# Attention on one core: VectorE takes the second maximum of a tile directly behind the first, ahead of the first low half

## What is computed

```python
x = x + _L0_xattn_ref(_layernorm(x), ctx_1024, ctx_1024, mask_SxS2_bk1, ...)   # masked
x = x + _L0_ffn_ref(_layernorm(x), ...)          # top 4 of 32 experts and a shared one
x = x + _L1_xattn_ref(_layernorm(x), ctx_1024, ctx_1024, ...)                  # not masked
x = x + _L1_ffn_ref(_layernorm(x), ...)          # three dense layers
# inside an attention, for each head:
scores = einsum('bhqd,bhkd->bhqk', Q, K) * 0.25
probs  = softmax(scores, axis=-1)
ctx    = einsum('bhqk,bhkd->bhqd', probs, V)
out    = ctx @ W_o + b_o
```

## Time and profile before

| what | value |
| --- | --- |
| median of 3 runs | 1339.29 us |
| the profiled execution | 1338.2 us, its span 1336.5 us |
| TensorE (matmuls) busy | 1172.4 us, 88% of the span |
| TensorE (weight loads) busy | 811.5 us, 61% |
| VectorE busy | 768.7 us, 58% |
| ScalarE busy | 521.4 us, 39% |
| GpSimd busy | 434.9 us, 33% |
| mean granted TensorE clock | 0.942 of full speed |
| steady part of the masked attention | 92.4 to 238 us |
| steady part of the second attention | 838 to 970 us |

### The profile page before, as it was taken

The page is one execution under the profiler, slowest core; times in us unless marked ns, Lnnn a source line. Parts: engine busy times, 40 slices in busy tenths (PEclk is TensorE's granted clock), DMA queues, the critical chain, the costliest instruction groups (busy, mean ns, idle before and its releaser), DMA issues. The chain is left out here.

```text
span 1336.5 us, 27175 instructions
## 1 busy us (share of the span) xinstructions
PE 1172.4 (88%) x8528; PEld 811.5 (61%) x8528; DVE 768.7 (58%) x2032; ACT 521.4 (39%) x1049; POOL 434.9 (33%) x559
## 2 busy tenths in 40 slices
PE   7789999789867199999998177999989999999998
PEld 4367777555544088888886034878755455554554
DVE  4257777868764066667665693888872434334331
ACT  6545555333230035544543165565641222212221
POOL 5221111167777455565555262222110000000000
PEclk9889999978889599999999588999999999999999
DMA  8199100026247355555452840000000000000000
GB/s 181 25 310 388 55 1 2 25 84 120 92 164 268 131 170 162 158 169 170 151 158 59 340 170 13 2 1 1 2 0 1 16 17 17 1 16 16 16 16 16
DMA packets 100740, 123.77 MB, mean 93 GB/s; under 512 B 33984, under 2 KB 76051, under 8 KB 100631
## 3 DMA queue, kind: packets, MB, share of 16 engines
q1 hardware_dynamic: 86807, 87.98, 22.1%
q0 software_dynamic: 13824, 34.38, 7.2%
HBM read 61.78 MB, written 64.72 MB: 95 GB/s over the span
## 5 line engine op out<-in xcount | busy, mean ns | idle before, releaser
L1871 PE MATMUL psA<-H,B 128*128 128x512 f16 x1024 | 223.5, 379 | 0.0
L1798 DVE SCALAR_TENSOR_TENSOR H<-psA,H 128x512 f16<-128x512 f32 x128 | 88.3, 690 | 208.3 <-ACT H L1839 208.3
L1557 POOL DMA_INDIRECT y_rows<-YB,pair x160 | 155.5, 972 | 119.7 <-issue 62.3
L1839 ACT ACTIVATE H<-psA 128x512 f16<-128x512 f32 x128 | 76.4, 597 | 252.7 <-PE psA L1871 252.7
L1871 PEld LDWEIGHTS psA<-H,B 128*128 128x128 f16 x1024 | 100.0, 98 | 119.5
L1667 PE MATMUL psH<-W,XT 128*128 x640 | 166.1, 382 | 0.0
L1230 POOL DMA_INDIRECT x_rows<-XN,slot_s x128 | 130.8, 1022 | 51.0 <-issue 45.1
L871 ACT ACTIVATE PHT<-psT 128x512 f16<-128x512 f32 (+1 forms) x192 | 93.6, 521 | 121.1 <-PE psT L931 121.0
L812 DVE TENSOR_REDUCE mx<-psS 128x8 fp32r<-128x616 f32 x128 | 101.4, 794 | 51.7 <-PE psS L910 49.9
L819 DVE TENSOR_TENSOR PLT<-psT,PHT 128x512 f16<-128x512 f32 (+1 forms) x192 | 109.3, 596 | 24.0 <-ACT PHT L871 24.0
L1667 PEld LDWEIGHTS psH<-W,XT 128*128 128x128 f32 x640 | 110.1, 192 | 8.8 <-issue 0.3
(11 more groups left out here) (250 smaller groups left out, 2069.5 us busy)
## 6 DMA issues: line engine op xcount, KB each, us to landing
XG<-x_rows SPq DMA_DIRECT2D x160, 134.0 KB, 2.5
y_rows<-zero_row SPq DMA_DIRECT2D x4, 4096.0 KB, 27.3
G<-y_rows SPq DMA_DIRECT2D x7, 2048.0 KB, 10.2
x_rows<-zero_row SPq DMA_DIRECT2D x33, 134.0 KB, 2.9
X<-in_x SPq DMA_DIRECT2D x8, 512.0 KB, 7.1
QT<-in_w SPq DMA_DIRECT2D x1, 4096.0 KB, 17.6
out_x<-OUT SPq DMA_DIRECT2D x8, 512.0 KB, 2.9
y_rows<-YB,pair POOLq DMA_INDIRECT x160
```

The lines of the kernel that those rows point to most:

```text
L1557: pool.indirect_dma_start(y_rows[:, :], bass.IndirectOffsetOnAxis(ap=pair[u // HALF][:, u % HALF:u % HALF + 1], axis=0), YB[u][:], None, b ...
L1798: dve.scalar_tensor_tensor(out=H[layer][1][:, o], in0=psA[k % 4][:], scalar=0.0, in1=H[layer][0][:, o], op0=ALU.max, op1=ALU.subtract).the ...
L1871: last = pe.matmul(psA[k % 4][:], W[:, c, o * P:(o + 1) * P], src[part][:, c], start=n == 0, stop=n == 2 * n_in - 1)
```

## The change

VectorE's `maximum` of half 1 moves from behind `low(t, 0)` to directly behind `maximum` of half 0. All else stays: no instruction is added or removed, the same semaphores are waited for, and the orders of TensorE and ScalarE are the same. It holds for all 32 tiles of both attentions, but for the first tile, whose two maxima were adjacent already.

```diff
@@ VectorE's body(t, u) in attend @@
                     if ok(t + 1):
                         maximum(t + 1, 1 - u, 0)
+                        maximum(t + 1, 1 - u, 1)
                     if ok(t):
                         low(t, u, 0)
-                    if ok(t + 1):
-                        maximum(t + 1, 1 - u, 1)
                     if ok(t - 3):
                         residual(t - 3)
                     if ok(t):
```

## The result

The changed kernel takes 1320.30 us (median of 4 runs, 1318.33 to 1321.65) against 1337.88 us (median of 4), a ratio of 0.9863 with a 95% interval of 0.9849 to 0.9877: 17.6 us or 1.4% faster. The forecast was a saving of 10 us, to 1329.3 us, and its range went from 1325 to 1337 us; the direction was right and the size too small. The profiled execution has a span of 1317.8 us, 18.7 us less.

The account below looks back on a forecast made before the run. TensorE sets the pace, its second shift waiting for VectorE's second maximum. Savings of 3.6 (masked), 5.9 (second) and 1.5 (first steps) less 1.0 us (last steps) give 10.0 us: 1329.3 us, range 1325 to 1337.

Parts of the forecast that it names:

- the stall of the second shift: TensorE's weight load of the second shift waits for VectorE's second maximum, about 0.47 us a step; forecast to vanish there.
- M + 1.42: New earliest start of low(t, 0), 1.42 us behind the start of the step's first maximum; before, 1.14 or 1.21 us.
- by full durations: Counter-reading on VectorE: each instruction starts after the previous one's full duration; low half 0.17 us later, no change to measure.
- the sum: TensorE's piece per step, first maximum to turn_context, from start-to-start distances: 2.90 us masked, 2.82 us second, against 3.045 us.
- The distance from low half to transposes: From the low half's end to the third group's first transpose: 0.14 us masked, 0.06 us second attention.
- M to C: Start of a step's first maximum to turn_context's first transpose on TensorE: 3.045 us before, forecast 2.90 masked and 2.82 second.
- The first steps: Start of the attentions: three steps at 0.35 us, with three ordinary ones at 0.15 us, 1.5 us gained in all.
- The last steps: Two in each attention, where VectorE works for the next stage: low half later, loss between 0 and 1.4, taken as 1.0 us.
- all other links shift along: Claim that the step's other links, such as second exponential and next scores, hang on TensorE's position and move with it.
- the whole stall: Rival: the low half comes no later, so 51 steps save 0.47 us each, 24 us, to 1315 us; chance 0.03.
- No change: Rival: saved wait used up by a 0.55 us second shift or VectorE instructions end to end; 1335.3 to 1343.3 us; chance 0.13.
- slower: Rival: third group's transposes and second shift don't overlap on TensorE, about 5 us more, 1344 us; chance 0.06.

Follow-up runs that it names:

- the short maximum: Against the kernel before, VectorE's old order kept, the second maximum of each tile reads 8 of 77 keys (a probe, no replacement): ratio 0.9839.
- the adjacent shifts: Against the changed kernel, TensorE's second shift moved ahead of the third group's transposes, directly behind the first shift: ratio 0.9842 to the kernel before, 1319.60 us.
- the adjacent exponentials: Against the kernel with the adjacent shifts, ScalarE's second exponential directly behind the first, ahead of the third high half, both attentions: 0.9794 to before, 1315.67 us.

## Why the prediction was wrong in size

- **The mechanism** was right: the stall of the second shift is gone, the low half starts at M + 1.42 in both attentions, the transposes wait instead, and the two maxima stand 0.71 us apart. The reading of the Trainium skill, page "VectorE: DVE Perf Modes", section "The DRAIN you can't avoid", by full durations (the low half at M + 1.59) is refuted by the same row: 147.41 against 145.99. The same section goes on that a next operation that is not held starts earlier. The prediction did not weigh that, and the trace agrees with it: the second maximum starts 0.08 us before the recorded end of the first in every steady step.
- **The step that failed** is the sum "low half 0.69 us; then 0.14 us (masked) or 0.06 us (second) to the first transpose; two transposes 0.23 us; the shift to `turn_context` 0.42 us". The last two terms were 0.51 to 0.54 us together instead of 0.65. I had said that the second shift straight behind the transposes isn't seen in the trace, and bounded it from above only, at 0.55 us; "from below 0.42 us, as behind the wait" was no lower bound but the length with a cost of the wait in it. The kernel with the short maximum shows the piece at 0.51 us in the old order as well. On average it is 0.525 us, so the sum had 0.125 us too much in each of 51 steps, 6.4 us.
- **The distance from low half to transposes** is not one for each attention, as the sum has it (0.14 masked, 0.06 second), but 0.11 us on average in both. It is 0.06 us behind the maxima of the tiles 11 to 14, 19 to 22, 27 and 28, before the change too; these are the steps that TensorE's program runs in its loop. (That program writes out the first and the last steps of every sequence of eight tiles, while those of VectorE and ScalarE loop from t = 4 to 27.) In the steps written out, and in the one round that the loop makes for the first sequence (tiles 5 and 6), it is 0.15 us. The steps shown in the earlier trace rows were one of each kind. This cost the sum 25 x 0.03 = 0.8 us in the masked attention and gave 26 x 0.05 = 1.3 us in the second, which nearly cancel.
- With these M to C is 2.74 us in both attentions instead of 2.90 and 2.82, which gives 0.31 us a step against 0.145 and 0.225. The steady stretches measured 7.6 / 25 = 0.30 and 8.8 / 26 = 0.34 us. In the second attention another 0.03 us came behind C: from there to the next scores it is 1.11 us before and 1.08 us after.
- **The first steps** of the masked attention gained 2.5 us and not 0.8 (3.1 in the profiled pair, of which 0.6 is not the order's), as one step went from the lower to the higher level of the clock. The forecast priced them by durations alone.
- **The last steps** were charged with 1.0 us of loss and gained 0.4 us: VectorE sets them, and TensorE's delay is nearly hidden, the possibility that I had named and not taken.
- **The statement that all other links shift along** held in the changed kernel, but only just. With M to C at 2.74 us the masked step is held by ScalarE's chain: the 2.51 us of the short maximum brought only 0.04 us more, the 2.58 us of the adjacent shifts 0.01 us, and the adjacent exponentials 0.22 us on top.
- **The rivals**: the whole stall (24 us) did not come back, though the short maximum, which does take it all away, gives 0.35 and 0.44 us a step, less than the 0.47 us of waits. No change and slower can be ruled out; the overlap of transposes and shift is larger, not smaller, than assumed.

What stays open is why a shift behind a wait needs 0.42 us to the next start and one in a running queue 0.34 to 0.35 us; the starts are recorded, the ends of matmuls modelled, and no run took this apart further. It is open as well why the distance from low half to transposes goes with TensorE's loop.

## What to carry to other kernels

A wait that ends in an in-order queue should be followed to the instruction that waits next, and the piece between them priced for a queue that flows. A distance taken from behind a stall may be too long (here 0.42 us against 0.34 to 0.35), so the range needs a lower bound from elsewhere, say the pace of the same kind of instructions within a run. And a distance that is read in one step should be read in the written-out steps and in the loop before it is multiplied by the number of steps. After one stall is moved, a kernel with the suspected work made short (here a maximum over 8 keys) tells how much is left to gain; where its step is not shorter though the queue has been freed, another engine sets it.

## What was unexpected of the hardware

- The same two shift products take 0.42 us to the next start when a wait held them and 0.34 to 0.35 us when none did, at the same clock.
- The delay from the end of the low half to the transposes that wait for it is 0.06 us in the steps of TensorE's loop that run two rounds and 0.15 us in the written-out ones, with the same instructions, before and after the change and in both attentions.
- A gain of 0.47 us in a step at the beginning of a stage became 1.6 us, as the step ran at the higher level of TensorE's clock (four products in 0.69 instead of 1.20 us), in all four traces that have the new order there and are otherwise as before.
